# Order of the first loads, x in pairs over the items, constants on VectorE, and all 48 weight pieces ahead of the first attention item

## What is computed

```python
x = x + tanh(g_xattn[0]) * xattn0(layernorm(x), ctx, ctx, mask, Wq, bq, Wk, bk, Wv, bv)
x = x + tanh(g_ffn[0])   * ffn0(layernorm(x), router_w, gate_w, up_w, down_w)
x = x + tanh(g_xattn[1]) * xattn1(layernorm(x), ctx, mask_bk)
x = x + tanh(g_ffn[1])   * ffn1(layernorm(x), gate_up_proj, down_proj)
# xattn0: per item 8 heads of width 8 over 256 x 256 scores, softmax, times v
# ffn0: softmax router over 8 experts with top-p 0.9; for each expert e
#   out += w[:, e] * ((silu(x @ gate_w[e].T) * (x @ up_w[e].T)) @ down_w[e].T)
# gate_w, up_w: 8 x 512 x 256 (float32); down_w: 8 x 256 x 512
```

## Time and profile before

| | |
|---|---|
| median of three runs | 1007.66 us |
| lowest, highest | 1003.5, 1012.44 us |
| profiled execution: time, span of its instructions | 1013.97, 1012.2 us |
| mean granted TensorE clock | 0.905 of full speed |
| PE, DVE busy | 81%, 77% |
| ACT, POOL busy | 57%, 56% |

### The profile page before, as it was taken

One profiled execution on the slowest core, in us unless ns is written; L12 is line 12 of the kernel. 1 busy time (PEld: TensorE's weight loads), 2 busy tenths in 40 slices (PEclk: granted clock), 3 DMA queues, 4 the chain that ended last, 5 costly groups with the idle time before them and its releaser, 6 DMA issues.

```text
span 1012.2 us, 24981 instructions
## 1 busy us (share of the span) xinstructions
PE 815.8 (81%) x9015; PEld 700.1 (69%) x9015; DVE 779.4 (77%) x2496; ACT 580.8 (57%) x1258; POOL 566.8 (56%) x565
## 2 busy tenths in 40 slices
PE   2445656889999999989999899999999688865564
PEld 2334444778888887878878788887788577754553
DVE  4385778898988989889898889989895686655652
ACT  2265777767777776676767577776673132222222
POOL 3253646777787776868777687877563122221110
PEclk9555676999999999999999999999999799987787
DMA  3759999786777887687877867678760400000100
GB/s 126 212 115 222 228 222 198 150 143 127 142 138 140 154 155 142 128 131 147 144 150 145 142 120 147 145 134 144 121 111 12 131 26 12 22 22 22 43 12 21
DMA packets 319520, 122.67 MB, mean 121 GB/s; under 512 B 274716, under 2 KB 312612, under 8 KB 319396
## 3 DMA queue, kind: packets, MB, share of 16 engines
q1 hardware_dynamic: 318656, 120.53, 59.6%
q10 hardware_dynamic: 740, 0.54, 0.2%
HBM read 45.53 MB, written 8.39 MB: 53 GB/s over the span
## 4 chain that ended last, share of the span: by engine, by line
PE 45%; DVE 20%; DMA 12%; issue 10%; ACT 5%; POOL 4%; SPq 3%; POOLq 0%; DVEq 0%; ACTq 0%
PE psU L754 11%; PE psG L754 10%; PE psY L754 8%; DMA p_turn<-p_parts 7%; PE psV L754 4%; PE ps L754 4%; DVE ps L1098 3%; PE psT L754 2%; DVE th_ga_h L1193 2%; PE psM L754 2%; POOL p_parts L530 2%; DMA stage<-in_L_ffn_up_w 2%; DMA stage<-in_L_ffn_gate_w 2%; PE psV L911 2%; DVE psT L1098 1%
## 5 line engine op out<-in xcount | busy, mean ns | idle before, releaser
L530 POOL TENSOR_TENSOR p_parts<-p,p_parts 128x512 f16<-128x512 f32 x256 | 297.6, 1165 | 169.3 <-ACT p_parts L636 155.6
L522 POOL TENSOR_TENSOR hp_lo<-th_ga_h,hp_hi 128x512 f16<-128x512 f32 x128 | 149.3, 1166 | 121.5 <-ACT hp_hi L660 119.0
L754 PE MATMUL psU<-xT,w_gu 128*128 128x256 f16 x1536 | 190.2, 274 | 30.7 <-DVE th_ga_h L1193 29.7
L754 PE MATMUL psG<-xT,w_gu 128*128 128x256 f16 x1536 | 194.4, 278 | 1.3 <-DVE th_ga_h L1185 1.3
L754 PE MATMUL psY<-w_dn,hp_hi 128*128 128x256 f16 x1024 | 183.8, 275 | 1.1 <-POOL hp_lo L522 1.1
L754 PEld LDWEIGHTS psU<-xT,w_gu 128*128 128x128 f16 x1536 | 142.4, 98 | 53.6 <-DVE th_ga_h L1193 37.5
L636 ACT ACTIVATE p_parts<-p 128x512 f16<-128x512 f32 x256 | 161.3, 630 | 27.6 <-DMA p_turn<-p_parts 26.3
L754 PEld LDWEIGHTS psG<-xT,w_gu 128*128 128x128 f16 x1536 | 146.3, 99 | 21.0 <-DVE th_ga_h L1185 1.4
L628 ACT ACTIVATE p<-psT,exp_bias 128x256 f32<-128x256 f32 x256 | 107.8, 475 | 71.2 <-DVE exp_bias L1102 55.7
L754 PE MATMUL psY<-w_dn,hp_lo 128*128 128x256 f16 x512 | 140.4, 274 | 0.0
L628 ACT ACTIVATE p<-ps,exp_bias 128x256 f32<-128x256 f32 x256 | 107.7, 475 | 57.0 <-DVE exp_bias L1102 55.2
(11 more groups left out here) (164 smaller groups left out, 1171.9 us busy)
## 6 DMA issues: line engine op xcount, KB each, us to landing
mask_in<-in_mask_Bx2048x_ff SPq DMA_DIRECT2D x32, 256.0 KB, 3.1
part_scratch<-parts SPq DMA_DIRECT2D x16, 384.0 KB, 3.2
q_stack<-part_scratch SPq DMA_DIRECT2D x62, 96.0 KB
k_stack<-part_scratch SPq DMA_DIRECT2D x62, 96.0 KB
stage<-in_L_ffn_gate_w SPq DMA_DIRECT2D x8, 512.0 KB, 5.0
stage<-in_L_ffn_up_w SPq DMA_DIRECT2D x8, 512.0 KB, 4.8
stage<-in_L_ffn_down_w SPq DMA_DIRECT2D x8, 512.0 KB, 4.5
p_turn<-p_parts SPq DMA_TRANSPOSE x256, 3.5
```

The source lines that it names most:

```text
L522: pool.tensor_tensor(hp_lo[:, u % 2, :], hb32[:, u % 2, :], hp_hi[:, u % 2, :], ALU.subtract).then_inc(s["h_split"], 1)
L530: pool.tensor_tensor(p_parts[:, g % 4, 1, :, :], p32[:, g % 2, :, :], p_parts[:, g % 4, 0, :, :], ALU.subtract).then_inc(s["plo_done"], 1)
L754: return pe.matmul(out_, lhsT, rhs, start=start, stop=stop, skip_group_check=shares_bank)
```

## The change

The first loads come in another order, with x's pairs 0 and 1 first and stage 0 and 1 of the weights ahead of the first mask. The rest of x comes two pairs at a time: pairs 2 and 3 in the lead, then two pairs in each fourth step (n % 4 == 2), and their statistics are taken on DVE in slot 3 of steps 0, 4, 8 to 24, the power on POOL in slot 5. DVE sets both halves of `q_stack`, `k_stack` and `v_parts` at its start. All 48 pieces are made in the lead: two between the first two projections, two more behind the second, the others behind the ACT queue's stack loads. ACT issues the load of stage c + 3 right behind the second `w_high` of stage c; SP issues only stages 0 to 2.

```diff
-W_AHEAD = 8
+W_AHEAD = 48
...
             if q < 2:
-                eng.wait_ge(s["stacks_set"], 2)
-                eng.wait_ge(s["q_zeroed"], q + 1)
+                eng.wait_ge(s["stacks_set"], 3)
...
+        def load_weight_stage(eng, c):
+
+            e, m = c // 3, c % 3
+            if e:
+                eng.wait_ge(s["wgrp_T"], 2 * (c - 3) + 2)
+            if m < 2:
+                src = A[("L0_ffn_gate_w", "L0_ffn_up_w")[m]][e].rearrange("(t p) h -> p t h", p=P)
+                dst = stage[m].rearrange("p (t h) -> p t h", t=IB)
+            else:
+                src = A["L0_ffn_down_w"][e].rearrange("(t p) i -> p t i", p=P)
+                dst = stage[m].rearrange("p (t i) -> p t i", t=2)
+            eng.dma_start(dst, src).then_inc(s[f"stage{m}_loaded"], 16)
...
+            def load_x(r):
+                sp.dma_start(x_res[:, r:r + 2, :], x_d[:, r:r + 2, :]).then_inc(s["x_loaded"], 16)
...
-                    if i % 2 == 0 and 6 + g // 2 < 3 * NE:
-                        load_weight_stage(6 + g // 2)
+                    if (n % 4, i) == (2, 4) and n + 6 <= NPAIR * 2 - 2:
+                        load_x(n // 2 + 3)
...
+            sp.dma_start(x_res[:, 0:2, :], x_d[:, 0:2, :]).then_inc(s["x01_loaded"], 16)
             load_small_weight(0, "wst_loaded")
             load_small_weight(1, "wst_loaded")
-            sp.dma_start(x_res[:, 0:2, :], x_d[:, 0:2, :]).then_inc(s["x01_loaded"], 16)
             sp.dma_start(ctx_in[:, 0, :], ctx_d[0]).then_inc(s["ctx0_loaded"], 16)
+            load_weight_stage(sp, 0)
             load_small_weight(2, "wv_loaded")
+            load_weight_stage(sp, 1)
+            sp.dma_start(ctx_in[:, 1, :], ctx_d[1]).then_inc(s["ctx1_loaded"], 16)
             load_mask(0, 0)
-            for c in range(3):
-                load_weight_stage(c)
-            sp.dma_start(ctx_in[:, 1, :], ctx_d[1]).then_inc(s["ctx1_loaded"], 16)
-            load_mask(1, 1)
+            load_weight_stage(sp, 2)
             store_parts(0, 0)
             for piece in range(2):
                 load_stacks(sp, 0, 0, piece)
-            sp.dma_start(x_res[:, 2:16, :], x_d[:, 2:16, :]).then_inc(s["x_loaded"], 16)
+            load_mask(1, 1)
+            load_x(2)
             store_parts(1, 1)
-            for c in range(3, 6):
-                load_weight_stage(c)
             sp.wait_ge(s["v_projected"], 1)
             sp.dma_start(ctx_in[:, 0, :], ctx_d[2]).then_inc(s["ctx0_loaded"], 16)
...
-            pool.memset(k_stack[:, :, :, :, :], 1.0).then_inc(s["stacks_set"], 1)
-            pool.memset(v_parts[:, :, :, :, :], 1.0).then_inc(s["stacks_set"], 1)
-            pool.wait_ge(s["stacks_set"], 2)
+            pool.wait_ge(s["stacks_set"], 3)
...
+            def pow1(r):
+                pool.wait_ge(s["ln1_in"], r // 2)
+                pool.tensor_tensor(rstd[:, r:r + 2], rstd[:, r:r + 2], minus_half[:, 0:2], ALU.pow).then_inc(s["pow1_done"], 1)
...
+                    if (n % 4, i) == (0, 5) and q + 2 < NPAIR:
+                        pow1(q + 2)
...
+                if k == 1 and 3 * e + m + 3 < 3 * NE:
+                    load_weight_stage(act, 3 * e + m + 3)
...
             copy_qk(0)
+            for w in range(2):
+                w_high(w // 6, w % 6 // 2, w % 2)
             copy_qk(1)
+            for w in range(2, 4):
+                w_high(w // 6, w % 6 // 2, w % 2)
             act.wait_ge(s["gate_loaded"], 32)
             act.activation(gates[:, :], gate_in[:, :], ACT.Tanh).then_inc(s["gates_ready"], 1)
-            for w in range(W_AHEAD // 2):
-                w_high(w // 6, w % 6 // 2, w % 2)
             for piece in range(2, 4):
                 load_stacks(act, 0, 0, piece)
-            for w in range(W_AHEAD // 2, W_AHEAD):
+            for w in range(4, W_AHEAD):
                 w_high(w // 6, w % 6 // 2, w % 2)
...
             pe.wait_ge(s["bias_ready"], 6)
             project_qk(0, 0)
+            for w in range(2):
+                weight_transposes(w // 6, w % 6 // 2, w % 2)
             pe.wait_ge(s["qk_copied"], 2)
             project_v(0, 0)
             pe.wait_ge(s["v_copied"], 1)
             project_qk(1, 1)
-            for w in range(W_AHEAD):
+            for w in range(2, W_AHEAD):
                 weight_transposes(w // 6, w % 6 // 2, w % 2)
...
             dve.sem_inc(s["w_split"], 2)
-            dve.memset(q_stack[:, 0, :, :, :, :], 0.0).then_inc(s["q_zeroed"], 1)
+            dve.memset(q_stack[:, :, :, :, :, :], 0.0).then_inc(s["stacks_set"], 1)
+            dve.memset(k_stack[:, :, :, :, :], 1.0).then_inc(s["stacks_set"], 1)
+            dve.memset(v_parts[:, :, :, :, :], 1.0).then_inc(s["stacks_set"], 1)
...
+                elif q % 2 == 0:
+                    dve.wait_ge(s["pow1_done"], q // 2)
...
-            dve.memset(q_stack[:, 1, :, :, :, :], 0.0).then_inc(s["q_zeroed"], 1)
             for w in range(W_AHEAD):
                 w_low(w // 6, w % 6 // 2, w % 2)
...
-                    if (n, i) == (0, 0):
-                        dve.wait_ge(s["x_loaded"], 16)
-                    if n == 0 and i < 7:
-                        norm1_stats(2 + 2 * i, 4 + 2 * i)
-                    if (n, i) == (0, 6):
-                        norm1_var(2, NPAIR, s["ln_in"])
+                    if (n % 4, i) == (0, 3) and q + 2 < NPAIR:
+                        dve.wait_ge(s["x_loaded"], 16 * (q // 2 + 1))
+                        norm1_stats(q + 2, q + 4)
+                        norm1_var(q + 2, q + 4, s["ln1_in"])
```

More of the change, by code:

```diff
@@ L126, in build @@
         bd = sb("bd", [P, P], F32)
-        names = """x01_loaded ln01_in pow01_done stacks_set q_zeroed bias_set bias_turned biasT_ready x_loaded
+        names = """x01_loaded ln01_in pow01_done stacks_set bias_set bias_turned biasT_ready x_loaded
             wst_loaded wv_loaded brow_loaded bias_v_loaded gate_loaded rt_loaded stage0_loaded stage1_loaded stage2_loaded ctx0_loaded ctx1_loaded
@@ L131, in build @@
             v_copied x1_done lg_done y_used x3_done d_upT wst_T router_T wgrp_T
-            w_split bias_ready ln_in pow_done xn_ready qk_projected v_projected qk_copied w_hi
+            w_split bias_ready ln_in pow_done ln1_in pow1_done xn_ready qk_projected v_projected qk_copied w_hi
             qk_split v_split scores_done max_done bias_done exp_done p_turned0 p_turned1 p_turned2 p_turned3 stack1_loaded phi_done plo_done pv_done
@@ L316, in load_small_weight @@
                              w_in[w].unsqueeze(1).broadcast_to([S, 2, S])).then_inc(s[done], 16)
-            def load_weight_stage(c):
-                e, m = c // 3, c % 3
-                if e:
-                    sp.wait_ge(s["wgrp_T"], 2 * (c - 3) + 2)
-                if m < 2:
-                    src = A[("L0_ffn_gate_w", "L0_ffn_up_w")[m]][e].rearrange("(t p) h -> p t h", p=P)
-                    dst = stage[m].rearrange("p (t h) -> p t h", t=IB)
-                else:
-                    src = A["L0_ffn_down_w"][e].rearrange("(t p) i -> p t i", p=P)
-                    dst = stage[m].rearrange("p (t i) -> p t i", t=2)
-                sp.dma_start(dst, src).then_inc(s[f"stage{m}_loaded"], 16)
+            def load_x(r):
+                sp.dma_start(x_res[:, r:r + 2, :], x_d[:, r:r + 2, :]).then_inc(s["x_loaded"], 16)
             def load_mask(b, slot):
@@ L509, in _ @@
             pool.wait_ge(s["bd_ready"], 3)
-            def pow1():
-                pool.wait_ge(s["ln_in"], 1)
-                pool.tensor_tensor(rstd[:, 2:16], rstd[:, 2:16], minus_half[:, 2:16], ALU.pow).then_inc(s["pow_done"], 1)
+            def pow1(r):
+                pool.wait_ge(s["ln1_in"], r // 2)
+                pool.tensor_tensor(rstd[:, r:r + 2], rstd[:, r:r + 2], minus_half[:, 0:2], ALU.pow).then_inc(s["pow1_done"], 1)
             def pow2(pair):
-                pool.wait_ge(s["ln_in"], 2 + pair)
+                pool.wait_ge(s["ln_in"], 1 + pair)
                 pool.tensor_tensor(rstd2[:, :], ve2[:, :], minus_half[:, 0:1], ALU.pow).then_inc(s["pow_done"], 1)
@@ L533, in late_pow @@
             def late_pow(j, i):
-                pool.wait_ge(s["ln_in"], 1 + NPAIR + 2 * j + i + 1)
+                pool.wait_ge(s["ln_in"], NPAIR + 2 * j + i + 1)
                 pool.tensor_tensor(crs[:, :], cve[:, :], minus_half[:, 0:2], ALU.pow).then_inc(s["pow_done"], 1)
@@ L546, in step @@
                     g, hp, half = 8 * n + i, i // 2, i % 2
-                    if (n, i) == (0, 6):
-                        pow1()
+                    if (n % 4, i) == (0, 5) and q + 2 < NPAIR:
+                        pow1(q + 2)
                     if 1 <= g <= 8 * B:
@@ L1137, in norm2 @@
             def norm2(pair):
-                dve.wait_ge(s["pow_done"], pair + 2)
+                dve.wait_ge(s["pow_done"], pair + 1)
                 dve.wait_ge(s["qk_projected"], min(pair + 3, NPAIR))
@@ L1248, in late_norm @@
             def late_norm(j, i):
-                dve.wait_ge(s["pow_done"], 1 + NPAIR + 2 * j + i + 1)
```

(1 more changed line is left out.)

3 lines of the change are left out of this document (removed).

## The result

| | before | after |
|---|---|---|
| median of the runs on this chip | 1010.05 us (4 runs, 1003.5 to 1014.38) | 1023.79 us (4 runs, 1022.54 to 1026.8) |
| profiled execution, its span | 1013.97, 1012.2 us | 1024.47, 1022.7 us |
| mean granted TensorE clock | 0.905 | 0.891 |

The ratio is 1.0142, with a 95% interval of 1.0105 to 1.0179: the change made the kernel **slower by 1.4%**.

The account below looks back on a forecast made before the run. The prediction took PE to bound the unit steps and late weight stages the slots before them. Unit 0 5.2 us later plus 3.5 us of statistics, 8.7 us on 1007.66, gave 1016 us; range 1001 to 1031.

Parts of the forecast that it names:

- the slower outcome: Whole kernel: a time more than about 1%, 10 us, above the kernel before; chance 0.42.
- Start: Lead up to the first projection: starts at about 13.5 instead of 15.7 us, a gain of 2, between 0 and 3.
- To the stack loads: Lead up to stage 3's first transpose: at 31.5 instead of 42.81 us, 11.3 us gained.
- The loop: Weight stages in the lead: 20 bank loops of 2.5 us, stage 23's first transpose at 81.5 us, first maximum at 85.5.
- rival of a lead bound by its loads: Lead: landing of 5.8 us makes a loop 3.0 us, 10 us more, 1026 us; chance 0.15.
- The slots: Attention slots between first maximum and unit 0, without weights: 88.2 us instead of 121.7, bounds 72 to 74 and 98.
- a free slot is 1.6: Slots where SP loads no stacks: 1.6 us each, from a range of 1.5 to 1.6.
- The first rival: Slots ahead of unit 0 stay long: 1.9 us a free slot, 10 us more, 1026 us; chance 0.27.
- upper bound of 1.9: Free slots: 1.9 us each as POOL's cuts and the router's short waits add up, slots 98 us in all.
- Unit 0: End of the slots: unit 0 starts at 173.7 instead of 168.5 us, 5.2 us later.
- The statistics: x's statistics in slot 3 of steps 8, 12, 16, 20 and 24: 0.7 us each, 3.5 us more.
- The units: Steps from unit 0 on: bound by PE, can't give anything back; the change can only move unit 0 or slow them.

Follow-up runs that it names:

- e10_nocut: The changed kernel with POOL's cuts of q and k left out for pairs 2 to 15, so their attention is wrong; 1020.71 us (one time).
- e3_stats1: The changed kernel with x's statistics in slot 1 of each fourth step instead of slot 3; 1021.04 us, ratio 1.0107 to the kernel before.
- e6_stackact: The changed kernel with stack pieces 2 and 3 of each pair loaded by ACT instead of SP; 1016.92 us, ratio 1.0072 to the kernel before.
- e11_best: The changed kernel with 8 pieces ahead, statistics in slot 1 and stack pieces 2 and 3 on ACT; 988.76 us, ratio 0.9793 to the kernel before.
- e1_w8: The changed kernel with 8 instead of 48 pieces ahead, 40 pieces back in slots 0 to 39; 995.13 us, ratio 0.9845 to the kernel before.

## Why the prediction came out as it did

The forecast was 1016 us, within its bound of 1% from before; measured were 1023.8, slower by 1.4%. That is inside the range of 1001 to 1031, but by the prediction's own bound it is the slower outcome, to which it gave 0.42, and not the forecast's. Of the 7.8 us between the two, 2.4 are the scale: 1016 stands on three runs of the kernel before (1007.66), the result on four (1010.05). The mechanism was the one forecast: a longer lead, shorter slots and a small loss in the unit steps. Each of the three terms was sized too low, and their sum of +8.7 came out as +10.5 between the two profiled executions and +13.7 between the medians.

**Start.** First projection forecast at 13.5 us, measured 14.3. The timeline of the start after:

```profile
1.81 3.47 DVE L1060 MEMSET q_stack<- 128x4096 uint32 x1 [1.81 <-issue]
6.08 3.47 DVE L1061 MEMSET k_stack<- 128x4096 bf16 x1 [0.80 <-issue]
9.84 1.39 DVE L1062 MEMSET v_parts<- 128x1600 bf16 x1 [0.28 <-issue]
...
11.74 0.36 PE L769 MATMUL psY<-ident,p 64*128 64x64 f32 x1 [2.82 <-DMA p<-in_L_xattn_Wv]
...
13.79 0.41 DVE L1086 TENSOR_SCALAR xn<-x_res,mean_var,rstd 128x256 f32<-128x256 f32 x1 [0.83 <-POOL rstd L489]
```

The price of the ones by elements held: 3.47 us for 4096 bfloat16, as for 4096 words of zeroes. This is what the Trainium skill ("VectorE: DVE Perf Modes", section "Zero memsets can be issued as uint32") says of the type. By the page's clock of 0.96 GHz 4096 elements would be an estimated 4.3 us; the trace has 3.47. DVE is free at 11.3 instead of 9.9 us, since it starts 0.4 later than taken and idles 0.80 and 0.28 us between the fills, where I had nothing; its statistics and POOL's power for `xn` come behind. `xn` itself took 0.41 us, as taken (4.37 before). Wv, there at 11.7 us, came before it.

**To the stack loads.** Forecast 31.5 us for stage 3's first transpose, measured 29.37. ACT's six stack loads took the 4.4 us of the earlier trace rows, from 23.42 to 27.86 us, and 1.5 us later the bank was free. The prediction gives only the sum of this stretch, so which of its items was taken too large can't be told. The 2.1 us gained were given back by the loop, so that the first maximum came right by two misses that cancel, and not by two terms that were right.

**The loop.** Forecast 20 loops of 2.5, 50.0 us; measured 29.37 to 82.07, 52.7. Eighteen beats of 2.59 to 2.62, and one each of 2.78 and 3.24, the latter two on stages whose load was late (34.74 and 37.98 us above). I had weighted the 2.62 us of the lower level with the mean clock of the old lead; but that clock is of a lead with other work between the transposes, and in a stretch of transposes alone TensorE stayed at the lower level throughout. The first maximum came at 86.08 (forecast 85.5). The rival of a lead bound by its loads (3.0 us a loop) did not come true: a load of a stage took 3.9 us as the median on ACT's queue, and only two were waited for.

**The slots.** Forecast 88.2, measured 91.8: this is the term that failed most at unit 0. Pair 0 took 34.2 (forecast 34) and step 0, which SP's stack loads don't reach, 12.2, so that a free slot is 1.5 us: the floor was right, and so were the turns 3.4 us apart (101.62 and 105.02 us in SP's queue). Pair 1 took 37.3 instead of 35.3, step 4 and two slots 20.2 instead of 18.9. The failed step is "a free slot is 1.6" for the slots with a cut: I had priced POOL at 1.16 a slot from the earlier trace rows and left its cuts to the upper bound, while with a cut a slot takes 1.8 to 2.3 us of POOL, and e10_nocut shows 3.0 us of them in steps 2 and 4. How far this carries the 3.6 us is shown in part only. Without the cuts step 4 and the two slots take 18.9 us, the forecast to the tenth, but pair 1 still takes 36.9 (forecast 35.3), because step 3 grew; what holds it is open. The first rival, 1.9 us in each free slot, is not what happened in step 0, and POOL's cuts, which the prediction names for its upper bound of 1.9, account for a part of the later steps.

**Unit 0.** Forecast +5.2, measured +9.4: 0.6 from the first maximum, 3.6 from the slots.

**The statistics.** Forecast 5 x 0.7 = 3.5 us, measured 5 x 1.0, which e3_stats1 took back by moving them alone. The place was wrong: PE's idle time before psU is still 0.76 us, and the new wait stands just ahead of it, before psV, for `pv_out`. The timeline of step 8 after:

```profile
250.50 0.43 DVE L1067 BATCH_NORM_STATS2 stats<-x_res 128x6 f32<-128x256 f32 x1
...
251.12 1.15 POOL L521 TENSOR_TENSOR hp_lo<-th_ga_h,hp_hi 128x512 f16<-128x512 f32 x1
251.17 1.13 DVE L1071 TENSOR_SCALAR rstd<-mean_var 128x2 f32<-128x2 f32 x1
...
254.04 0.35 PE L757 MATMUL psV<-v_parts,p_turn 128*128 128x25 bf16 x8 [0.81 <-DVE o_rec L1126]
...
255.15 1.05 PE L757 MATMUL psU<-xT,w_gu 128*128 128x256 f16 x8 [0.76 <-DVE th_ga_h L1200]
```

The waits of the kernel after from 178 to 887 us (us in total, times, longest) have a row that those of before lack:

```profile
PE psV L757 <- DVE o_rec L1126: 4.1, 5, 0.9
```

The work was mis-sized too: I took 1.4 us for two rows and "a small one", but from 249.83 to 252.22 it is 2.4, because the small one on 2 columns took 1.13 us here, where it takes 0.17 in the lead. Its length is that of POOL's instruction beside it: in each of the five steps it starts 0.05 to 0.06 us after POOL's `hp_lo` and ends 0.02 to 0.03 us after that has ended. In slot 1 (e3_stats1) it took 0.56 to 0.58 us in four of the five steps, and ended within 0.03 us of POOL's `p_low`; in the fifth it started at the same moment as POOL's instruction and took 0.17. The `xn` of 4.37 us in the earlier trace rows, which ends at 15.64 us, 0.15 after POOL's second fill of ones, looks like the same case. So the prediction had the effect in view for the ones in the lead and left it out for the statistics. No run here separates what in the chip holds such an instruction.

**The units.** The prediction said that the steps with units are bound by PE and can't give anything back. They can: with half of the stack loads on ACT they took 702.3 us in e6_stackact and 696.6 in e11_best, both below the 703.8 to 716.5 of the kernels without this edit and with the statistics in slot 3, and against 706.5 before; and e6_stackact is 0.7% faster than the kernel after although its slots are 1 us longer. PE is idle for some 60 us of this stretch in the kernel before (706.6 less 647.0).

**The larger error is in what I compared.** The prediction summed the whole change and found a near balance. e1_w8 shows two large terms under it: the rest of the change gains 16.5 us at unit 0, and 40 pieces moved ahead of the slots lose 25.9. I had the gain of the lead (11.3 us at stage 3) but credited it to the loop that spent it, and asked of the slots only how short they become, not what the same pieces cost there.

## What to carry to other kernels

Work that has a dependent chain of its own (here transposes, high part, low part over two banks) costs its full latency where it stands alone, here 1.3 us a piece, and 0.3 to 0.6 us where it fills gaps of other work; moving it ahead of a stage is only worth it if the stage then shrinks by more than the chain's latency. Separate, by one run each, the parts of a change that load earlier from those that move work: here the first alone are 1.5% faster and hid a loss of 26 us. When an engine is given a few small instructions, price each slot with all that the engine has in that slot, not with a mean, and look at what another engine runs beside them.
